# The tile's own layer norm taken in columns through a DRAM round trip, g's parts in one instruction, and a written-out order for the last tile

## The chip, the cores and the metric

One core of one Trainium2 chip runs the whole program. The metric is the device time of one execution in microseconds (us), as the median of several; a profiled execution of the same kernel has a time of its own and a span, from its first to its last instruction.

## The reference

There are 10,000 rows `x` of width 128 and a 10,000 x 10,000 matrix `adj`. Cut to what matters:

```python
h = item_feat @ W_item.T + b_item
x = x + relu(adj @ h + layernorm(x) @ W_user.T + b_user)     # x1
xn = layernorm(x)                                            # the tile's own normalisation
probs = softmax(xn @ gate_w + gate_b); cw = top-2 of probs, 0 elsewhere
x = x + sum_e cw[:, e] * (gelu(xn @ W1[e] + b1[e]) @ W2[e] + b2[e])     # 8 experts, hidden 256
```

The layer norm takes mean and variance over the 128 features of a row and has an eps of 1e-5.

## The kernel before

Everything is held transposed: features lie in the 128 partitions and rows of `x` in columns. The 10,000 rows are cut into 20 tiles of T = 500 columns. One pass of the program multiplies one tile by all of `adj`'s columns, in NPOS = 40 positions. A position 0 to 38 has two blocks of 128 rows of `adj` and three matmuls for each block (high x high, high x low, low x high, since values are split in two fp32r parts), six in all; position 39 has one. ScalarE makes the high part `a_hi` of what the DMA put into `raw` (line 456), VectorE the low part `a_lo` (line 599), TensorE uses both (lines 819 to 821). `raw` and `a_lo` have 8 buffers, `a_hi` has 4, so ScalarE can be at most three positions ahead of TensorE, and SyncE issues the load of a position when TensorE has finished the position eight before it.

The rest of the work, the tail of a tile, is woven into the positions of the next pass, by tables: `tail(i, p)` and `experts(i, p)` on each engine do a step when `p` has the position named at the top of the file (`T_`, `STARTS`, `DOWNS` for TensorE; `A_` for ScalarE; `V_`, `SCALES`, `ADDS` for VectorE; `S_` for SyncE). Positions of 40 and more of a table belong to the following pass. Each engine runs its instructions in the order in which its positions come, and waits at each for semaphores. At one position the order is: the part of `adj`, the tail of this tile, the experts left over from the tile before, the experts of this tile, and the steps of the next tile's `user` normalisation.

The tail of a tile before the change:

- ScalarE takes relu of `acc` into `r_sb` (481), VectorE adds `x_sb` into `x1_sb` (652), TensorE turns `x1_sb` into rows in `ps_v` with four transposes (854, `T_TURN`).
- VectorE takes mean and variance of the rows (612 to 621), GpSimd the power -0.5 (418), VectorE normalises the rows into `xt_sb` with four instructions (625), and TensorE turns them back into columns in `ps_x` with four transposes (827, `T_BACK`).
- ScalarE copies `ps_x` into `xn_hi` (485), VectorE makes `xn_lo` (661), ScalarE copies `ps_x` into `xn_sb` (488), TensorE multiplies that with the gate's weights (863), and the softmax and the ranking of the top two run on VectorE and ScalarE (668 to 710, 491). The weights go to DRAM (495) and come back, spread over all partitions, as `spread_sb` (374).
- For each expert TensorE makes `ps_z` (878 to 880, three matmuls for each of two halves; called up below), ScalarE gelu in `g_sb` (505) and its high part `g_hi` (511), VectorE the low part `g_lo` (718), TensorE the product into `ps_y` (844 to 846, six matmuls; called down below), and VectorE the scaled `t_sb` (727) and the sum `o_sb` (741). `g_sb` has two buffers of two halves.

The `user` normalisation of the next tile's `x` already goes the other way: its means and roots are turned by one small VectorE transpose, stored in DRAM (`u_moments_rows`, 474) and read back spread over all partitions (353, 354), and the columns are normalised in place by a subtraction and a product (642, 644).

After the twentieth pass there is no further pass to weave into: all engines go through the same tables with no `adj` work between.

## Time and profile before

| | |
|---|---|
| time, median of 3 runs | 1610.36 us (1608.63 to 1611.47) |
| profiled execution: its time | 1609.19 us |
| its span | 1607.3 us |
| TensorE matmul busy (PE) | 1585.5 us, 99% |
| TensorE weight loads busy (PEld) | 1310.9 us, 82% |
| VectorE busy (DVE) | 1497.5 us, 93% |
| ScalarE busy (ACT) | 1247.6 us, 78% |
| mean granted TensorE clock | 0.998 |

In a profile the engines are PE and PEld (TensorE's matmuls and weight loads), DVE (VectorE), ACT (ScalarE), POOL (GpSimd) and SP (SyncE); a name with q is an engine's queue, at which it issues DMAs. A busy time counts a stretch in which two matmuls overlap once, and one matmul of 500 columns lasts longer than the distance to the next; so what an instruction costs the engine is read from the starts of its neighbours in the timeline.

### The profile page before, as it was taken

To read this page: it belongs to the slowest core of one execution; us is meant where nothing else is said; L and a number is where in the kernel's file an instruction comes from. 1 tells how busy PE (TensorE), PEld (TensorE's weight loads), DVE (VectorE), ACT (ScalarE), POOL (GpSimd) and SP (SyncE) were. 2 spreads that over 40 slices of the span, in tenths; PEclk is the share of its full clock that TensorE was granted. 3 is DMA by queue.
4 is the path that set the end of the run, shared out by engine and by line. 5 is a ranking of instruction groups with operands and counts; after the bars stand their busy time and mean duration, and the time that the engine had idled before them with its cause. 6 is when DMAs were issued, how large, how long until landed. Compare 5 with 4: busy or idle time off the path is not lost.

```text
span 1607.3 us, 26715 instructions
## 1 busy us (share of the span) xinstructions
PE 1585.5 (99%) x7165; PEld 1310.9 (82%) x7165; DVE 1497.5 (93%) x2328; ACT 1247.6 (78%) x1597; POOL 86.0 (5%) x63
## 2 busy tenths in 40 slices
PE   8999999999999999999999999999999999999996
PEld 7878888888888888888888888888888888888875
DVE  6989999999999999999999999999999999999987
ACT  5777877787878787878787777878787878787765
POOL 2000000000000000000000000000000000000000
PEclk9999999999999999999999999999999999999999
DMA  9999898989898989898989889898989898989851
GB/s 375 359 335 324 271 333 283 318 287 319 285 318 286 316 280 320 289 318 291 314 298 305 301 301 304 297 317 288 315 278 338 265 333 269 332 278 324 281 176 65
DMA packets 159974, 477.75 MB, mean 297 GB/s; under 512 B 22817, under 2 KB 55458, under 8 KB 159954
## 3 DMA queue, kind: packets, MB, share of 16 engines
q1 hardware_dynamic: 150816, 469.37, 86.0%
q10 hardware_dynamic: 8306, 5.84, 1.1%
q0 software_dynamic: 832, 2.30, 0.4%
q8 instruction: 10, 0.16, 0.0%
q14 instruction: 10, 0.08, 0.0%
HBM read 471.66 MB, written 5.78 MB: 297 GB/s over the span
## 4 chain that ended last, share of the span: by engine, by line
issue 92%; PE 4%; POOL 2%; DVE 1%; ACT 1%; DMA 0%; POOLq 0%; ACTq 0%; DVEq 0%
POOL moments_sb L418 2%; PE acc L819 1%; PE acc L821 1%; PE acc L820 1%; ACT g_sb L505 0%; DVE g_lo L718 0%; DMA w_item_sb<-in_w_itemT 0%; PE ps_v L790 0%; DVE o_sb L741 0%; PE ps_y L790 0%; PE ps_g L790 0%; ACT a_hi L456 0%; PE ps_z L790 0%; PE ps_y L844 0%; DVE a_lo L599 0%
## 5 line engine op out<-in xcount | busy, mean ns | idle before, releaser
L456 ACT ACTIVATE a_hi<-raw 128x1000 fp32r<-128x1000 f32 (+1 forms) x800 | 811.8, 1027 | 257.1 <-PE acc L821 202.3
L599 DVE TENSOR_TENSOR a_lo<-raw,a_hi 128x1000 fp32r<-128x1000 f32 x780 | 916.2, 1193 | 57.8 <-ACT a_hi L456 56.3
L819 PE MATMUL acc<-a_hi,h_hi 128*128 128x500 f32 x1560 | 610.4, 391 | 2.3 <-DVE a_lo L599 1.5
L821 PE MATMUL acc<-a_hi,h_lo 128*128 128x500 f32 x1560 | 608.1, 390 | 0.0
L820 PE MATMUL acc<-a_lo,h_hi 128*128 128x500 f32 x1560 | 605.6, 388 | 0.0
L819 PEld LDWEIGHTS acc<-a_hi,h_hi 128*128 128x128 f32 x1560 | 293.5, 188 | 62.8 <-issue 3.5
L820 PEld LDWEIGHTS acc<-a_lo,h_hi 128*128 128x128 f32 x1560 | 294.1, 189 | 59.3
L821 PEld LDWEIGHTS acc<-a_hi,h_lo 128*128 128x128 f32 x1560 | 293.3, 188 | 59.8
L505 ACT ACTIVATE g_sb<-ps_z,b_sb 128x500 f32<-128x500 f32 x320 | 197.9, 670 | 38.9 <-PE ps_y L846 30.3
L718 DVE TENSOR_TENSOR g_lo<-g_sb,g_hi 128x500 fp32r<-128x500 f32 x320 | 201.8, 672 | 7.2 <-ACT g_hi L511 7.2
L511 ACT ACTIVATE g_hi<-g_sb 128x500 fp32r<-128x500 f32 x320 | 179.3, 611 | 0.0
L878 PE MATMUL ps_z<-xn_hi,w_hi 128*128 128x500 f32 x320 | 126.8, 396 | 1.6 <-ACT g_sb L505 1.6
L844 PE MATMUL ps_y<-g_hi,w_hi 128*128 128x500 f32 x312 | 122.2, 392 | 5.0 <-DVE g_lo L718 5.0
L880 PE MATMUL ps_z<-xn_hi,w_lo 128*128 128x500 f32 x320 | 125.0, 391 | 0.0
L879 PE MATMUL ps_z<-xn_lo,w_hi 128*128 128x500 f32 x320 | 124.7, 390 | 0.0
L845 PE MATMUL ps_y<-g_lo,w_hi 128*128 128x500 f32 x312 | 122.0, 391 | 0.0
L846 PE MATMUL ps_y<-g_hi,w_lo 128*128 128x500 f32 x312 | 121.7, 390 | 0.0
L727 DVE SCALAR_TENSOR_TENSOR t_sb<-ps_y,b_sb,spread_sb 128x500 f32<-128x500 f32 x156 | 114.1, 732 | 0.0
L418 POOL TENSOR_TENSOR moments_sb<-var_sb,power_sb 128x4 f32<-128x4 f32 x20 | 37.8, 1888 | 1234.4 <-DVE var_sb L621 1234.4
L741 DVE TENSOR_TENSOR o_sb<-o_sb,t_sb 128x500 f32<-128x500 f32 x140 | 94.2, 673 | 1.0
L844 PEld LDWEIGHTS ps_y<-g_hi,w_hi 128*128 128x128 f32 x312 | 59.2, 190 | 19.4 <-issue 7.4
L878 PEld LDWEIGHTS ps_z<-xn_hi,w_hi 128*128 128x128 f32 x320 | 60.3, 188 | 17.2 <-issue 4.4
(126 smaller groups left out, 878.0 us busy)
## 6 DMA issues: line engine op xcount, KB each, us to landing
raw<-in_adj_main SPq DMA_DIRECT2D x780, 500.0 KB, 5.3
spread_sb<-scales SPq DMA_DIRECT2D x160, 250.0 KB, 6.1
xr_sb<-in_xR SPq DMA_DIRECT2D x20, 256.0 KB, 5.4
x_sb<-in_xT SPq DMA_DIRECT2D x20, 250.0 KB, 5.0
xr_sb<-u_moments_rows SPq DMA_DIRECT2D x20, 250.0 KB, 5.4
r_sb<-u_moments_rows SPq DMA_DIRECT2D x20, 250.0 KB, 6.7
out<-o_sb ACTq DMA_DIRECT2D x20, 250.0 KB, 5.9
items<-in_itemT SPq DMA_DIRECT2D x13, 384.0 KB, 8.2
```

The source lines that it names most:

```text
L456: nc.scalar.activation(a_hi[q][0:rows, 0:cols], raw[s][0:rows, 0:cols], ACT.Copy).then_inc(hi_ready, 1)
L505: nc.scalar.activation(g_sb[e % 2][j][:, :], ps_z[j][:, 0:T], ACT.Gelu, bias=b1_sb[:, e * HH + j:e * HH + j + 1]).then_inc(gelu_ready, 1)
L511: nc.scalar.activation(g_hi[e % 2][j][:, :], g_sb[e % 2][j][:, :], ACT.Copy).then_inc(g_hi_ready, 1)
L599: nc.vector.tensor_tensor(low, whole, val(high), ALU.subtract).then_inc(lo_ready, 1)
L718: nc.vector.tensor_tensor(g_lo[e % 2][j][:, :], g_sb[e % 2][j][:, :], val(g_hi[e % 2][j][:, :]), ALU.subtract).then_inc(g_lo_ready, 1)
L819: nc.tensor.matmul(acc[:, 0:T], w_hi, m_hi, start=(k == 0), stop=False)
L820: nc.tensor.matmul(acc[:, 0:T], w_hi, m_lo, start=False, stop=False)
L821: last = nc.tensor.matmul(acc[:, 0:T], w_lo, m_hi, start=False, stop=False)
L844: nc.tensor.matmul(y, w2_hi[:, cols], hi, start=(j == 0), stop=False)
L878: nc.tensor.matmul(ps_z[j][:, 0:T], w1_hi[:, at:at + P], xn_hi[:, :], start=True, stop=False)
L879: nc.tensor.matmul(ps_z[j][:, 0:T], w1_hi[:, at:at + P], xn_lo[:, :], start=False, stop=False)
L880: nc.tensor.matmul(ps_z[j][:, 0:T], w1_lo[:, at:at + P], xn_hi[:, :], start=False, stop=True).then_inc(z_done, 1)
```

## The change

The tile's own normalisation goes the way of the `user` one. VectorE transposes the 32 columns of means and roots (`turned_sb[1]`), ScalarE stores them in a new DRAM tensor `t_moments_rows` (`A_MOMENTS`), SyncE reads the means into `xt_sb` and the roots into `r_sb`, spread over all partitions (`S_TAIL`), and VectorE makes `xn_sb` from `x1_sb` in two instructions (`V_XN`). The four row instructions, TensorE's four transposes back and ScalarE's copy into `xn_sb` are gone; `xn_hi` and `xn_lo` are made from `xn_sb`. The two halves of `g_sb`, `g_hi` and `g_lo` become one tile each, and high and low part take one instruction of 1000 columns in place of two of 500. The tables have new positions. The first two DMAs on ScalarE's queue change places. For the last tile `g` gets four buffers, in `raw`, `a_lo` and `a_hi`, and each engine's order after the last pass is written out.

```diff
-T_TURN, T_BACK, T_GATE = 1, 9, 13
-U_DENSE = 38
-STARTS = (15, 21, 24, 30, 37, 39, 43, 49)
-DOWNS = (21, 28, 35, 38, 43, 45, 51, 55)
-SCALES = (34, 37, 40, 42, 48, 51, 55, 61)
-ADDS = (36, 40, 41, 42, 51, 54, 58, 62)
+T_TURN, T_GATE = 0, 15
+U_DENSE = 37
+STARTS = (13, 20, 23, 28, 34, 39, 42, 48)
+DOWNS = (20, 24, 35, 40, 42, 45, 51, 58)
+SCALES = (35, 36, 38, 42, 48, 52, 59, 60)
+ADDS = (36, 37, 41, 46, 50, 56, 60, 61)
-S_SPREAD = (34, 34, 34, 35, 42, 45, 49, 54)
+S_SPREAD = (36, 36, 36, 36, 43, 44, 46, 50)
-A_RELU, A_NORM, A_XN, A_EXP, A_SEND, A_STORE, A_USER, A_FFN, A_SCALED = 2, 13, 15, 17, 28, 30, 17, 4, 6
-V_X1, V_STATS, V_NORM, V_LO, V_USTATS, V_UTURN, V_UNORM, V_SCALED = 2, 4, 6, 12, 10, 14, 33, 6
-S_USER = 26
-V_LOGITS, V_PROB, V_COMPARE, V_RANK, V_WEIGHT = 15, 18, 20, 22, 24
+A_RELU, A_MOMENTS, A_NORM, A_EXP, A_SEND, A_STORE, A_USER, A_FFN, A_SCALED = 1, 5, 13, 22, 28, 30, 17, 4, 5
+V_X1, V_STATS, V_NORM, V_XN, V_LO, V_USTATS, V_UTURN, V_UNORM, V_SCALED = 1, 2, 3, 11, 13, 8, 11, 31, 5
+S_TAIL, S_USER = 13, 25
+V_LOGITS, V_PROB, V_COMPARE, V_RANK, V_WEIGHT = 20, 22, 23, 24, 25
...
+            def spread_tail(i, p):
+                if p == S_TAIL:
+                    sp.wait_ge(t_stored, i * 16)
+                    sp.dma_start(xt_sb[:, 0:T], columns(t_moments_rows, 0)).then_inc(t_spread, 16)
+                    sp.dma_start(r_sb[:, :], columns(t_moments_rows, 2)).then_inc(t_spread, 16)
...
+            act.dma_start(w_item_sb[:, :], w_itemT).then_inc(w_item_landed, 16)
             act.dma_start(b_item_raw[0:1, 0:D], b_item).then_inc(b_item_landed, 16)
-            act.dma_start(w_item_sb[:, :], w_itemT).then_inc(w_item_landed, 16)
...
                 if p == V_NORM:
                     dve.wait_ge(t_rstd, i)
-                    normalise(1, xt_sb[0:TQ, :], ps_v[0:TQ, :], t_normed)
+                    since(dve, t_stored, i * 16 - 16)
+                    nc.vector.transpose(turned_sb[1][:, :], moments_sb[1][:, :]).then_inc(t_squared, 1)
+                if p == V_XN:
+                    dve.wait_ge(t_spread, i * 32)
+                    dve.wait_ge(relu_ready, i)
+                    nc.vector.tensor_tensor(xn_sb[:, 0:T], x1_sb[:, 0:T], xt_sb[:, 0:T], ALU.subtract).then_inc(t_less, 1)
+                    dve.wait_ge(t_less, i)
+                    nc.vector.tensor_tensor(xn_sb[:, 0:T], xn_sb[:, 0:T], r_sb[:, :], ALU.mult).then_inc(xn_ready, 1)
...
+            def low(i, e):
+                g, hi, lo = g_places(i)
+                dve.wait_ge(g_hi_ready, expert(i, e) + 1)
+                nc.vector.tensor_tensor(lo[e % len(g)][:, :], g[e % len(g)][:, :], val(hi[e % len(g)][:, :]),
+                                        ALU.subtract).then_inc(g_lo_ready, 1)
```

The written-out end, TensorE's part of it (`rest` is tile 19's leftover, NB tile 20):

```diff
+            tail(NB, T_TURN)
+            down(rest, 3)
+            down(rest, 4)
+            up(rest, 6)
+            down(rest, 5)
+            up(rest, 7)
+            down(rest, 6)
+            tail(NB, T_GATE)
+            up(NB, 0)
+            down(rest, 7)
+            up(NB, 1)
+            up(NB, 2)
+            down(NB, 0)
...
+            down(NB, 5)
+            down(NB, 6)
+            down(NB, 7)
```

VectorE's order there begins with the sum of `rest`'s expert 2, then `x1`, the statistics, the scaling of 3, the small transpose, the scaling of 4; after `V_XN` come the scaling of 5, the logits, the sum of 5 and `xn_lo`. It ends with the scaling and sum of 6 and the scaling and sum of 7. ScalarE's has relu, gelu and high part of 5, the store of the moments, and alternates gelu and high part for the rest.

## Rows read from the trace of the kernel before

**Rows 1.** Waits of the steady passes: engine, line, releaser; us, times, longest.
```profile
PEld acc L819 <- DVE a_lo L599: 1.0, 4, 0.4
```
**Rows 2.** Timeline of TensorE at two pass ends: start us, duration, instruction.
```profile
777.14 1.00 PE L834 MATMUL acc<-xn_sb,w_user_sb 128*128 128x500 f32 x2
...
854.89 1.00 PE L834 MATMUL acc<-xn_sb,w_user_sb 128*128 128x500 f32 x2
```
**Rows 3.** Timeline of TensorE around the four transposes back.
```profile
797.46 0.39 PE L821 MATMUL acc<-a_hi,h_lo 128*128 128x500 f32 x1
797.69 0.60 PE L827 MATMUL ps_x<-ident_sb,xt_sb 128*128 128x128 f32 x4
798.04 0.47 PE L878 MATMUL ps_z<-xn_hi,w_hi 128*128 128x500 f32 x1
798.36 0.39 PE L879 MATMUL ps_z<-xn_lo,w_hi 128*128 128x500 f32 x1
```
**Rows 4.** Timeline of VectorE in the same pass.
```profile
782.38 1.26 DVE L718 TENSOR_TENSOR g_lo<-g_sb,g_hi 128x500 fp32r<-128x500 f32 x2
...
789.52 1.36 DVE L625 TENSOR_SCALAR xt_sb<-ps_v,moments_sb 128x128 f32<-128x128 f32 x4
...
839.57 0.68 DVE L642 TENSOR_TENSOR xn_sb<-x_sb,xr_sb 128x500 f32<-128x500 f32 x1
```
**Rows 5.** Costliest groups of the page: busy, mean ns of one, idle before.
```profile
L456 ACT ACTIVATE a_hi<-raw 128x1000 fp32r<-128x1000 f32 (+1 forms) x800 | 811.8, 1027 | 257.1 <-PE acc L821 202.3
L599 DVE TENSOR_TENSOR a_lo<-raw,a_hi 128x1000 fp32r<-128x1000 f32 x780 | 916.2, 1193 | 57.8 <-ACT a_hi L456 56.3
...
L505 ACT ACTIVATE g_sb<-ps_z,b_sb 128x500 f32<-128x500 f32 x320 | 197.9, 670 | 38.9 <-PE ps_y L846 30.3
...
L727 DVE SCALAR_TENSOR_TENSOR t_sb<-ps_y,b_sb,spread_sb 128x500 f32<-128x500 f32 x156 | 114.1, 732 | 0.0
```
**Rows 6.** Waits of SyncE's queue, whole span: us, times, longest.
```profile
SPq L105 <- DMA scales<-cwT_sb: 14.1, 17, 1.6
```
**Rows 7.** Timeline: the weights' store and the first reads of it.
```profile
827.87 0.53 ACTq L495 DMA_DIRECT2D scales<-cwT_sb  x1
...
833.12 1.39 SPq L374 DMA_DIRECT2D spread_sb<-scales  x3
```
**Rows 8.** DMA issue of the page: KB each, median us to landing.
```profile
r_sb<-u_moments_rows SPq DMA_DIRECT2D x20, 250.0 KB, 6.7
```
**Rows 9.** Windows, after the last pass: length, busy (count), then clock, DMA.
```profile
1555.80:1573.70 17.90, 13.82 (x59) 10.15 (x58) 15.16 (x40) 11.03 (x19) 1.37 (x1) 0.91 0.04 15
```
**Rows 10.** Timeline after the last pass.
```profile
1557.82 0.47 PE L878 MATMUL ps_z<-xn_hi,w_hi 128*128 128x500 f32 x1
...
1568.61 1.06 PE L863 MATMUL ps_g<-gate_w_sb,xn_sb 128*128 128x8 f32 x8 [0.99 <-ACT xn_sb L488]
...
1573.71 0.51 PE L878 MATMUL ps_z<-xn_hi,w_hi 128*128 128x500 f32 x1
...
1581.36 0.54 ACTq L495 DMA_DIRECT2D scales<-cwT_sb  x1
...
1583.32 0.80 SPq L374 DMA_DIRECT2D spread_sb<-scales  x2
...
1601.94 0.39 PE L846 MATMUL ps_x<-g_hi,w_lo 128*128 128x500 f32 x1
...
1604.68 0.35 ACTq L516 DMA_DIRECT2D out<-o_sb  x1
```
**Rows 11.** DMA issues in the stretch after the last pass.
```profile
spread_sb<-scales SPq DMA_DIRECT2D x9, 250.0 KB, 3.3
```
**Rows 12.** Timeline of the start.
```profile
0.75 0.55 ACTq L434 DMA_DIRECT2D xn_sb<-in_b_item  x1
...
1.33 0.37 ACTq L435 DMA_DIRECT2D w_item_sb<-in_w_itemT  x1
...
5.56 1.65 PE L790 MATMUL ps_v<-w_item_sb,items 128*128 128x128 f32 x6 [5.56 <-DMA w_item_sb<-in_w_itemT]
```

More of the change, by code:

```diff
@@ L184, in build @@
         with ExitStack() as whole:
-            g_sb = [[whole.enter_context(nc.sbuf_tensor(f"g_sb{s}_{j}", [P, T], fp32)) for j in range(HH)] for s in range(2)]
-        g_lo = [[sb(f"g_lo{s}_{j}", [P, T], fp32r) for j in range(HH)] for s in range(2)]
+            g_sb = [whole.enter_context(nc.sbuf_tensor(f"g_sb{s}", [P, HH * T], fp32)) for s in range(2)]
+        g_lo = [sb(f"g_lo{s}", [P, HH * T], fp32r) for s in range(2)]
         with ExitStack() as first_pass:
@@ L288, in build @@
         b_item_raw = xn_sb
-        landing = [g_sb[0][0], g_sb[0][1], t_sb[1], x1_sb, o_sb]
+        landing = [g_sb[0][:, 0:T], g_sb[0][:, T:2 * T], t_sb[1], x1_sb, o_sb]
         def columns(rows, n):
@@ L540, in _ @@
                 one_pass(i, True, True)
-            for p in range(NPOS):
-                tail(NB, p)
-                experts(NB - 1, p + NPOS)
-                if p == A_STORE:
-                    finish(NB)
-                experts(NB, p)
-            for p in range(NPOS, 2 * NPOS):
-                experts(NB, p)
+            rest = NB - 1
+            tail(NB, A_RELU)
+            gelu(rest, 5)
+            high(rest, 5)
+            tail(NB, A_MOMENTS)
+            gelu(rest, 6)
+            high(rest, 6)
+            gelu(rest, 7)
+            tail(NB, A_NORM)
+            high(rest, 7)
+            tail(NB, A_EXP)
+            gelu(NB, 0)
+            high(NB, 0)
+            gelu(NB, 1)
+            tail(NB, A_SEND)
+            high(NB, 1)
+            gelu(NB, 2)
+            finish(NB)
+            high(NB, 2)
+            gelu(NB, 3)
+            high(NB, 3)
+            gelu(NB, 4)
+            high(NB, 4)
+            gelu(NB, 5)
+            high(NB, 5)
+            gelu(NB, 6)
+            high(NB, 6)
+            gelu(NB, 7)
+            high(NB, 7)
             finish(NB + 1)
@@ L731, in add @@
[L731 to L742 removed]
+                    low(i, STARTS.index(p - V_SCALED))
@@ L744, in one_pass @@
+                if p in SCALES:
+                    scale(i, SCALES.index(p))
+                if p in ADDS:
+                    add(i, ADDS.index(p))
             def one_pass(i, with_tail, with_finish):
@@ L764, in _ @@
                 one_pass(i, True, True)
-            for p in range(NPOS):
-                tail(NB, p)
-                experts(NB - 1, p + NPOS)
-                add(NB - 1, p + NPOS)
-                experts(NB, p)
-                add(NB, p)
-            for p in range(NPOS, 2 * NPOS):
-                experts(NB, p)
-                add(NB, p)
+            rest = NB - 1
+            add(rest, 2)
+            tail(NB, V_X1)
+            tail(NB, V_STATS)
+            scale(rest, 3)
+            tail(NB, V_NORM)
+            scale(rest, 4)
+            add(rest, 3)
+            low(rest, 5)
+            low(rest, 6)
+            add(rest, 4)
+            tail(NB, V_XN)
+            scale(rest, 5)
+            tail(NB, V_LOGITS)
+            add(rest, 5)
+            tail(NB, V_LO)
+            low(rest, 7)
+            scale(rest, 6)
+            tail(NB, V_PROB)
+            add(rest, 6)
+            tail(NB, V_COMPARE)
+            tail(NB, V_RANK)
+            tail(NB, V_WEIGHT)
+            low(NB, 0)
+            scale(rest, 7)
+            add(rest, 7)
+            low(NB, 1)
+            low(NB, 2)
+            scale(NB, 0)
+            scale(NB, 1)
+            add(NB, 0)
+            low(NB, 3)
+            scale(NB, 2)
+            add(NB, 1)
+            low(NB, 4)
+            add(NB, 2)
+            scale(NB, 3)
+            low(NB, 5)
+            add(NB, 3)
+            scale(NB, 4)
+            add(NB, 4)
+            low(NB, 6)
+            scale(NB, 5)
+            add(NB, 5)
+            low(NB, 7)
+            scale(NB, 6)
+            add(NB, 6)
+            scale(NB, 7)
+            add(NB, 7)
         @block.tensor
@@ L822, in adj_step @@
                 last.then_inc(adj_used, 1)
-            def back(rows, done):
-                for q in range(Q):
-                    last = nc.tensor.transpose(ps_x[:, q * TQ:(q + 1) * TQ], rows[0:TQ, q * D:(q + 1) * D],
-                                               ident_sb[0:TQ, 0:TQ])
-                last.then_inc(done, 1)
             def user(i, p):
```

160 lines of the change are left out of this document (77 added, 83 removed).

## The prediction

> **What bounds the kernel now.** I read first the busy shares of the page: TensorE 99%, VectorE 93%. A busy share alone doesn't name the bound, so the waits of the steady passes come next. Between the first and the last pass end TensorE's weight loads lose 1.0 us in all to a missing low part [rows 1]; VectorE's lateness costs nothing. So a steady pass is as long as TensorE's queue. Its length is the distance of the `user` matmuls at two pass ends, 854.89 - 777.14 = 77.75 us [rows 2]. One matmul of 500 columns costs 0.227 us from start to start (797.46 to 797.69 is 0.23), though it is shown 0.39 long [rows 3]; six of them, a position or an up or a down, cost 1.36. What TensorE no longer has to do shortens each pass; what the other engines save shortens nothing there. After the last pass it is different: in the first 17.9 us TensorE is busy 13.82, and the clock granted is 0.91 of full speed on the mean [rows 9]. There chains of waits decide. That end lasts from 1555.8 to the span's end at 1607.3, 51.5 us.
>
> **The steady passes: what goes.** The four transposes back start at 797.69, the next two matmuls at 798.04 and 798.36 [rows 3]. From 797.46 to 798.36 are 0.90 us, in which two matmuls alone would take 0.454. So the transposes cost 0.446 us a pass. They go in 19 passes outside the end: 19 x 0.446 = 8.5 us. The gate's, the turn's and the experts' matmuls stay, only at other positions. Here a rule of the Trainium skill can be weighed: the page "TensorE: Matmul & The Clock Gate" (section "Back-to-back issue gap") gives some 81 ns for each weight load and matmul of 128 columns in a stream. By it the estimate would be 4 x 0.081 x 19 = 6.2 us; no row here shows the 81 ns, and the row's 0.446 for four stands.
>
> VectorE, per pass: the four row instructions go (1.36 us [rows 4]); a subtraction and a product come, like the pair of `user`, 2 x 0.68 us [rows 4], and a small transpose (0.1 to 0.2 us); eight pairs of low parts become single instructions, 1.26 against 1.19 us [rows 4, 5], 0.56 saved. The net is -0.4 us (0.1 to 0.2 of the 1.36 is overlap with neighbours), about what TensorE's pass loses, so VectorE is as loaded as before. ScalarE loses a copy and gains a DMA issue of 0.53 us (as in [rows 7]); it is at 78% and its total is free.
>
> **The new waits in a pass.** I walk the new tables with position 0 of TensorE at time 0, a position, an up and a down at 1.36 us each. The chain is: relu, `x1`, turn at 1.4 to 1.8; statistics to 3.6; power on GpSimd; the small transpose at 5.7; ScalarE reaches position 5 at 6.5 (at position 3 it waits until 3.4 for `down` of expert 3, since `g_sb` has two buffers) and issues the store at about 7.5. What the store takes under load is the unknown. [Rows 7] bound it from above: 833.12 - 827.87 = 5.25 us for the like store of the weights, and SyncE was held by that one in 17 cases by 0.8 us on the mean [rows 6], so it is not much less. From below the quiet end gives 1583.32 - 1581.36 = 1.96 us [rows 10]. I take 5.25, as it is under the same traffic: 12.75. SyncE comes to position 13 when TensorE has ended position 5, at 12.9, so its wait costs it next to nothing, and the loads of `raw` queued behind are not late. It issues the two reads at 13.3 and 13.65; the root's takes 6.7 us in the median [rows 8]: 20.35. VectorE, loaded as it is, ends `a_lo` of position 11 at about 20.8. So the wait of `V_XN` just fits. Queued behind it is everything of VectorE, first `a_lo` 12, which by the walk is ready 1.1 to 1.5 us before TensorE wants it. The cover of the round trip is thus 0.45 + about 1.1 = 1.5 us.
>
> The second tight place is `DOWNS[1]` = 24, while the low part it needs stands at VectorE's position 25, behind `a_lo` 25 and `V_WEIGHT`. TensorE would start that down at 50.3. VectorE's queue from position 18 on, where it waits for ScalarE until 32.1, holds 8 `a_lo` at 1.11 us from start to start (1.19 long [rows 5] with the overlap of 0.08), three more pieces of `low`, scale and sum, and the gate's five steps (an estimate of 3.5 us together, from the starts of their neighbours in the same pass): it ends at 49.8. There are 0.5 us left. At the other places I find a microsecond or more: `up` 6 at 5.9 has its gelu at 4.6, `up` 5 at 75.9 its at 72.2. So I cost the new order at nothing in the likeliest case, with 0 to +0.5 us a pass as the range; a gain is excluded, since TensorE already waits for nothing.
>
> SyncE's two more reads are 0.5 MB on top of some 23 MB a pass, 2%; the DMA engines are busy 0.90 of the time there, and `raw` has its eight buffers in front. I cost it at nothing, and the landing of the reads above already stands in the traffic.
>
> **The start.** `w_item` moves from the second to the first place of ScalarE's queue, 1.33 to 0.75 us [rows 12]. TensorE's first matmul waits for it until 5.56; from there it is in a chain with TensorE busy nearly all of the first pass. Up to 0.58 us gained, nothing if another load is last; I take 0.5.
>
> **The end.** Before, the first `up` of tile 20 starts at 1573.71 and the last matmul at 1601.94 [rows 10]. New (in the times of the old run): the turn is over when TensorE's next matmul starts, 1557.8 [rows 10], the statistics come next in VectorE's written order, 1.5 us from 1558.15, and GpSimd's power takes 1.4 (its whole busy time in [rows 9]): 1561.1. But ScalarE is free for the store only after gelu and high part of expert 5. Gelu waits for `down` 3, which takes the matmul's place of 1557.8 and ends 1.6 later with its latency, 1559.45. Two halves of gelu at 0.62 from start to start (0.67 long) and a high part of 1.03 [rows 5] make 1561.75. The store takes 1.96 [rows 10]: 1563.7. The second read is issued at 1564.0 and lands 3.3 later [rows 11]: 1567.3. Subtraction and product to 1568.8, gate to 1569.9 (1.06 [rows 10]), logits 0.6, the sum of 5 0.6, `xn_lo` 0.6: 1571.9. So `up` 0 comes 1.8 us earlier although the round trip is long, since the old chain stood behind other work. From there TensorE has 17 pieces of 1.36 us (8 up, 9 down), 23.1 us; before it had 16, 21.8 us, and took 1602.3 - 1573.7 = 28.6. In the new order ScalarE needs per expert 2 x 0.62 + 1.03 = 2.3 us and VectorE 1.19 + 0.73 + 0.6 = 2.5, both under TensorE's 2.72, and four buffers keep them apart. What is left is the first gelu (table load and gelu to 1575.5, high and low part to 1577.6) against which `down` 7, `up` 1 and `up` 2 are set, and some small waits; by the walk the last down starts at 1596.35 and ends at 1597.8. After it come one scaling and one sum in place of a scaling and two sums: 1.6 us to 1599.4, and from the issue of the output 2.65 us as before (1607.3 - 1604.68 [rows 10]): 1602.05. That is 5.25 us less. TensorE still waits for the gate and for `xn_lo`, some 3 us with the gate's small matmuls between, as in the stretch whose mean clock was 0.91 [rows 9]. I expect the lower level of the two (1.2 GHz) again in `up` 0, which puts the first gelu 0.7 us later. So 4.6 us are left.
>
> **The sum.** 8.5 + 0.5 + 4.6 = 13.6 us. The profiled execution took 1609.2 us (span 1607.3, 1.9 around it), so the one after would take 1595.6, its span 1593.7. The median stands 1.2 above the profiled one: 1596.8. I say 1596.5.
>
> **The rivals.**
> - *The round trip is longer than its cover (slower side).* Place: `V_XN` at position 11, VectorE's whole queue behind it, TensorE's `a_lo` next. It decides from 1.5 us more than worked out above (a root landing after 21.9); each us beyond costs 19 us in all. To lose against before it needs 13.6 / 19 = 0.7 us more, 2.2 in all. With 3 us more: 1.5 x 19 = 28 lost, 1611. For it: the reads land between 6 and 8 us under load, and terms are in series. Against: 5.25 is an upper bound. 9%.
> - *The low part of expert 1 is late.* Place: TensorE's `down` 1. VectorE 0.9 us later than my walk costs 0.4 x 18 = 7 us: 1604. For it: VectorE is 93% busy and the margin is the thinnest. 14%.
> - *The end gives nothing:* a read that lands 2 us later, and half clock for longer, eat 4.6 us: 1601. 10%.
> - *The transposes cost their whole duration.* Were the 0.60 us shown for the group [rows 3] all TensorE's time, 19 x 0.60 = 11.4 would go in place of 8.5: 1593.9. Against it speaks the start of the next matmul 0.35 us after theirs. The page "TensorE: Matmul & The Clock Gate" of the Trainium skill (section "Part 4: PE-mode transpose") has "~275 ns" for one in a kernel; four in series, an estimate by it, would be 1.1 us a pass and 21 us in all. 3%.
> - *The change doesn't do what it says:* TensorE's time is freed and VectorE becomes the bound, 1605 to 1609, as VectorE's total shrinks no faster than the pass. Against: at 93% it has some 5 us of a pass idle. 3%.
>
> The forecast itself, 1592 to 1600, has 61%.
>
> **How the numbers follow.** The range leaves out most of the first rival, the upper end of the last and what the end may bring beyond the forecast: 1591.5 to 1606.5. Faster by over 0.2% (3.2 us, about what a measurement tells from no change) is all below 1607.1: forecast, third, fourth, most of the second and part of the last, 0.86. Same: 0.06. Slower, above 1613.6 or nearly: 0.08.
>
> **What would show it.** The distance between `user` matmuls should be 77.3 us; TensorE's waits in the passes still near nothing. Were the first rival true, VectorE's `xn_sb` from `x1_sb` would show a wait for the read of `t_moments_rows` in most passes and TensorE one for `a_lo`. The second shows as TensorE at `ps_y` waiting for `g_lo` once a pass. In the end, `up` 0 should start some 14 us after the first matmul behind the turn (1571.9 - 1557.8), and the last matmul some 26.5 us after `up` 0; a later `up` 0 makes the third rival. If VectorE's idle time falls to nothing while TensorE's waits grow, the last is true.

## The result and the profile after

The changed kernel takes 1598.41 us in the median of 6 runs (1597.69 to 1600.52), the old one 1609.62 (1608.63 to 1611.47, 6 runs). The ratio is 0.9933 with a 95% interval of 0.9923 to 0.9944: 11.2 us faster. The profiled execution of the changed kernel took 1598.9 us, its span is 1596.9 where the old span was 1607.3, so the two traces differ by 10.4 us. The forecast was 13.6 us between profiled executions and 1596.5 as the time.

The page of the changed kernel, busy time and share by engine:

```profile
PE 1575.2 (99%) x7085; PEld 1304.3 (82%) x7085; DVE 1491.0 (93%) x2148; ACT 1225.2 (77%) x1419; POOL 68.5 (4%) x63
```

TensorE has 80 matmuls fewer and VectorE 180 instructions fewer, yet the shares are what they were. So the shares don't say where the 10.4 us come from; marks on TensorE's queue do. As the mark of a pass I take the start of the pass's last `adj` matmul, L810 before and L892 after. Timeline of TensorE before, at the ends of passes 0, 1 and 19 (start us, duration, instruction):

```profile
85.96 0.78 PE L810 MATMUL acc<-a_hi,h_hi 128*128 128x500 f32 x1
...
155.51 0.79 PE L810 MATMUL acc<-a_hi,h_hi 128*128 128x500 f32 x1
...
1555.14 0.79 PE L810 MATMUL acc<-a_hi,h_hi 128*128 128x500 f32 x1
```

The same after, with the `user` pair (L909) of two passes:

```profile
87.09 0.38 PE L892 MATMUL acc<-a_hi,h_hi 128*128 128x500 f32 x1
...
158.09 0.39 PE L892 MATMUL acc<-a_hi,h_hi 128*128 128x500 f32 x1
...
773.59 1.00 PE L909 MATMUL acc<-xn_sb,w_user_sb 128*128 128x500 f32 x2
...
850.80 1.00 PE L909 MATMUL acc<-xn_sb,w_user_sb 128*128 128x500 f32 x2
...
1547.92 0.39 PE L892 MATMUL acc<-a_hi,h_hi 128*128 128x500 f32 x1
```

One thing has to be set right first. The matmul that follows the `user` pair takes 0.62 us to the next start, not 0.23 (774.04 to 774.66 after, 777.59 to 778.21 before). Before, the mark itself is that matmul; after, the pair stands a position earlier and the slow step lies ahead of the mark. So 0.39 us moves from behind the mark to ahead of it, in pass 0 as a loss that is none, in the end as a gain that is none. With that:

| stretch | before | after | difference | forecast |
|---|---|---|---|---|
| pass 0, to its mark | 85.96 | 87.09 | +1.13, less 0.39: +0.74 | -0.5 |
| pass 1 | 69.55 | 71.00 | +1.45 | -0.45 |
| passes 2 to 19 | 1399.63 | 1389.83 | -9.80 | -8.0 |
| mark to the span's end | 52.16 | 48.98 | -3.18, plus 0.39: -2.79 | -4.6 |
| sum | | | -10.4 | -13.6 |

The steady pass is 850.80 - 773.59 = 77.21 us, where it was 77.75 [rows 2]. The window of the steady passes after (length; busy time and count of PE, PEld, DVE, ACT and POOL; clock, DMA share, GB/s), and behind it the waits there (engine, line, releaser: us, times, longest), to set beside [rows 1]:

```profile
160.00:1547.00 1387.00, 1387.00 (x6199) 1148.86 (x6198) 1318.62 (x1888) 1081.17 (x1239) 52.58 (x36) 1.00 0.91 310
```
```profile
PEld acc L901 <- DVE a_hi L640: 0.2, 1, 0.2
```

TensorE has no gap in 1387 us. [Rows 1] shows one of two such lines of the old kernel; the other is

```profile
PEld acc L810 <- DVE a_lo L599: 1.6, 7, 0.2
```

The two cost nearly nothing: 16 of the old kernel's 18 passes from mark 1 to mark 19 are 77.75 us apart and two are 77.84 and 77.85, so the old pass too was as long as TensorE's queue.

The new round trip (store, two reads, `V_XN`) and the thin margin of `down` 1 in one steady pass, whose mark is at 775.79:

```profile
783.16 0.54 ACTq L502 DMA_DIRECT2D t_moments_rows<-turned_sb  x1
...
790.83 0.35 SPq L356 DMA_DIRECT2D xt_sb<-t_moments_rows  x1
791.24 0.42 SPq L357 DMA_DIRECT2D r_sb<-t_moments_rows  x1
...
797.94 0.67 DVE L697 TENSOR_TENSOR xn_sb<-x_sb,xt_sb 128x500 f32<-128x500 f32 x1
...
815.65 0.74 DVE L764 SCALAR_TENSOR_TENSOR t_sb<-ps_y,b_sb,spread_sb 128x500 f32<-128x500 f32 x1 [0.89 <-PE ps_y L922]
...
825.86 1.16 DVE L756 TENSOR_TENSOR g_lo<-g_sb,g_hi 128x1000 fp32r<-128x1000 f32 x1
...
827.68 0.39 PE L920 MATMUL ps_y<-g_hi,w_hi 128*128 128x500 f32 x1
```

With position 0 at 777.37, the reads leave at 13.5 and 13.9 (walked: 13.3 and 13.65) and `V_XN` starts at 20.6 (walked: 20.8). The store goes out at 5.8, not 7.5. The page gives 5.6 us from issue to landing of the root's read, not 6.7:

```profile
r_sb<-t_moments_rows SPq DMA_DIRECT2D x20, 250.0 KB, 5.6
```

With this median as an estimate the root is there at 796.84, 1.1 us ahead of `V_XN`, which waits for nothing. SyncE never waits for the store in these passes; it does so twice in the whole span, 0.3 us in pass 1 and 2.6 us in the end:

```profile
SPq L356 <- DMA t_moments_rows<-turned_sb: 2.9, 2, 2.6
```

The low part of expert 1 ends at 827.02, 0.66 us ahead of its down product (walked: 0.5).

Pass 1 is another matter. SyncE, VectorE and TensorE there, after:

```profile
95.28 0.49 PE L901 MATMUL acc<-a_hi,h_hi 128*128 128x500 f32 x1 [0.61 <-DVE a_lo L640]
...
98.94 0.33 SPq L356 DMA_DIRECT2D xt_sb<-t_moments_rows  x1
99.69 0.33 SPq L357 DMA_DIRECT2D r_sb<-t_moments_rows  x1
...
106.00 0.68 DVE L697 TENSOR_TENSOR xn_sb<-x_sb,xt_sb 128x500 f32<-128x500 f32 x1 [1.61 <-DMA r_sb<-t_moments_rows]
...
108.65 0.49 PE L901 MATMUL acc<-a_hi,h_hi 128*128 128x500 f32 x1 [2.08 <-DVE a_lo L640]
```

In a steady pass TensorE has ups and downs of the previous tile between its `adj` products (at positions 0 to 18), and VectorE gets ahead meanwhile. Pass 1 has no previous tile. From 100 to 125 us TensorE is idle 2.08 us, all in this last wait; before, it was idle 0.00 there.

The end after, in order of time:

```profile
1559.43 0.68 DVE L697 TENSOR_TENSOR xn_sb<-x_sb,xt_sb 128x500 f32<-128x500 f32 x1 [1.25 <-DMA r_sb<-t_moments_rows]
...
1560.88 1.06 PE L936 MATMUL ps_g<-gate_w_sb,xn_sb 128*128 128x8 f32 x8 [0.79 <-DVE xn_sb L699]
...
1563.89 0.76 PE L948 MATMUL ps_z<-xn_hi,w_hi 128*128 128x500 f32 x1 [1.95 <-issue]
...
1577.57 0.74 DVE L764 SCALAR_TENSOR_TENSOR t_sb<-ps_y,b_sb,spread_sb 128x500 f32<-128x500 f32 x1 [1.37 <-DMA spread_sb<-scales]
...
1588.55 0.47 PE L920 MATMUL acc<-a_hi,w_hi 128*128 128x500 f32 x1 [0.70 <-DVE a_lo L756]
...
1591.02 0.47 PE L920 MATMUL ps_x<-a_hi,w_hi 128*128 128x500 f32 x1 [0.86 <-DVE a_lo L756]
...
1592.22 0.38 PE L922 MATMUL ps_x<-a_hi,w_lo 128*128 128x500 f32 x1
...
1594.13 0.35 ACTq L535 DMA_DIRECT2D out<-o_sb  x1
```

`up` 0 follows the first matmul behind the turn (1550.20) by 13.7 us; 14 was forecast. From `up` 0 it is 28.3 us to the start of the last matmul and 28.7 to its end; some 26.5 was forecast. That is where the end fell short.

### The profile page after: what moved, and what is told of

Its sections match the earlier page's. It is cut to its first block, busy times and chain, and to the rows that moved or that the text cites. A ratio compares the mean times of both kernels' runs of the same rounds, so it can differ in the third digit from the quotient of the medians.

```text
span 1596.9 us, 26046 instructions
## 1 busy us (share of the span) xinstructions
PE 1575.2 (99%) x7085; PEld 1304.3 (82%) x7085; DVE 1491.0 (93%) x2148; ACT 1225.2 (77%) x1419; POOL 68.5 (4%) x63
## 4 chain that ended last, share of the span: by engine, by line
issue 93%; PE 2%; DMA 2%; POOL 1%; DVE 1%; ACT 0%; SPq 0%; POOLq 0%; DVEq 0%; ACTq 0%
POOL moments_sb L431 1%; DMA raw<-in_adj_main 1%; PE acc L901 0%; PE acc L903 0%; PE acc L902 0%; DMA spread_sb<-scales 0%; DVE t_sb L764 0%; DMA r_sb<-t_moments_rows 0%; DVE o_sb L775 0%; ACT a_hi L469 0%; DVE a_lo L640 0%; DVE a_lo L756 0%; DMA t_moments_rows<-turned_sb 0%; SPq L334 0%; PE ps_y L872 0%
## 5 line engine op out<-in xcount | busy, mean ns | idle before, releaser
L901 PE MATMUL acc<-a_hi,h_hi 128*128 128x500 f32 x1560 | 617.7, 396 | 6.3 <-DVE a_lo L640 5.5
L517 ACT ACTIVATE g_sb<-ps_z,b_sb 128x500 f32<-128x500 f32 x304 | 188.0, 669 | 61.9 <-PE ps_y L922 59.7
L756 DVE TENSOR_TENSOR g_lo<-g_sb,g_hi 128x1000 fp32r<-128x1000 f32 x152 | 181.0, 1191 | 5.2 <-ACT g_hi L523 5.1
L523 ACT ACTIVATE g_hi<-g_sb 128x1000 fp32r<-128x1000 f32 x152 | 156.3, 1028 | 0.1
L922 PE MATMUL ps_y<-g_hi,w_lo 128*128 128x500 f32 x304 | 118.2, 389 | 0.0
L431 POOL TENSOR_TENSOR moments_sb<-var_sb,power_sb 128x4 f32<-128x4 f32 x20 | 21.0, 1052 | 1211.7 <-DVE var_sb L662 1211.7
L949 PEld LDWEIGHTS ps_z<-xn_lo,w_hi 128*128 128x128 f32 x320 | 60.6, 189 | 12.2
```

Of the source, the lines that this page charges most:

```text
L517: nc.scalar.activation(g[e % len(g)][:, j * T:(j + 1) * T], ps_z[j][:, 0:T], ACT.Gelu, bias=b1_sb[:, e * HH + j:e * HH + j + 1]).then_inc( ...
L523: nc.scalar.activation(hi[e % len(g)][:, :], g[e % len(g)][:, :], ACT.Copy).then_inc(g_hi_ready, 1)
L756: nc.vector.tensor_tensor(lo[e % len(g)][:, :], g[e % len(g)][:, :], val(hi[e % len(g)][:, :]), ALU.subtract).then_inc(g_lo_ready, 1)
L901: nc.tensor.matmul(acc[:, 0:T], w_hi, m_hi, start=(k == 0), stop=False)
L949: nc.tensor.matmul(ps_z[j][:, 0:T], w1_hi[:, at:at + P], xn_lo[:, :], start=False, stop=False)
```

## The experiments

All but one start from the changed kernel. The steady pass is taken from the marks of passes 1 to 19 in one execution, where it nearly always repeats to 0.01 us as long as nothing waits. All times but the last kernel's are of single runs, the profiled ones, and are compared with the profiled execution of the changed kernel, 1598.9 us. Its parts outside the steady passes vary from one execution to the next, as shown below. The old kernel ran beside them in 1609.3 to 1610.0 us.

### The transposes back again

```diff
+                if p == 9 and not is_last(i):
+                    for q in range(Q):
+                        nc.tensor.transpose(ps_x[0:TQ, q * D:(q + 1) * D], x1_sb[:, q * TQ:(q + 1) * TQ], ident_sb[:, :])
```

> The changed kernel with four 128x128 transposes of x1 into the bank of the z product put back on TensorE at position 9 of passes 1 to 19, where the old kernel turned the normalised tile back; nobody reads or waits for them, so they cost TensorE's time alone. My account (TensorE's own work sets the steady pass, and the removed transposes were worth 0.446 us): the steady pass goes from 77.21 to 77.66 us, and the run by about 8.5 us, from 1598.4 to 1607. Rival (each transpose costs its whole 0.15 us duration, 0.60 for four): 77.81 us, and 1610. Rival (the gain came from a wait in the old path around the transposes, not from their own time): below 77.4 us, under 4 us in all.

1606.33 us, 7.4 more. Two marks in a row:

```profile
779.72 0.39 PE L892 MATMUL acc<-a_hi,h_hi 128*128 128x500 f32 x1
...
857.36 0.39 PE L892 MATMUL acc<-a_hi,h_hi 128*128 128x500 f32 x1
```

77.64 us, 0.43 more than without them. My account stands: the transposes cost TensorE what the starts around them show, 0.353 for the four and 0.085 more for the matmul behind them. 0.353 / 4 is 0.088 us each. The page "TensorE: Matmul & The Clock Gate" of the Trainium skill (section "Back-to-back issue gap") says some 81 ns, which comes near that but leaves out the slower matmul behind. The "~275 ns" of the same page of the Trainium skill (section "Part 4: PE-mode transpose") is three times what the rows show. But the old pass is 77.75: 0.11 us a pass, 2.0 us in 18, came from something else.

### A wait that is met, and g in two parts

The first puts eight waits a pass back on TensorE, the second also the 16 instructions that the merging took away.

```diff
                 for j in range(HH):
+                    if j:
+                        pe.wait_ge(g_lo_ready, expert(i, e) + 1)
```

> The changed kernel with one more semaphore wait on TensorE ahead of the second half of each expert's down product, for a count that has always been reached: eight more waits a pass, as many as the old kernel had. The steady pass got 0.535 us shorter where the transposes explain 0.446. Theory A (each wait costs TensorE about 11 ns even when its count is reached): the steady pass goes from 77.21 to 77.30 us, the run by 1.6 us. Theory B (a wait that is met costs nothing, and the 0.09 came from elsewhere): 77.21 us, no change.

```diff
...
+                for j in range(HH):
+                    part = slice(j * T, (j + 1) * T)
+                    dve.wait_ge(g_hi_ready, i * (E * HH) + (HH * (e - E) + j + 1))
+                    nc.vector.tensor_tensor(lo[e % len(g)][:, part], g[e % len(g)][:, part], ...
...
```

> The changed kernel with the high and the low part of g made in two instructions of 500 columns each again, each with a wait and a signal of its own, and TensorE waiting for each low part, as in the old kernel; all else as changed. It puts 8 instructions a pass on ScalarE and 8 on VectorE back, and TensorE's 8 waits. Theory A (the merged instructions give TensorE the 0.09 us a pass by its waits): steady pass 77.30 us, VectorE's busy share up by about 1 us a pass with no new wait. Theory B (it comes from elsewhere): 77.21 us. Rival: VectorE gets so late that down 1, with its margin of 0.66 us, waits in each pass: over 77.5 us, with a wait of ps_y for g_lo in the rows.

1599.78 and 1599.12 us; the marks are 77.21 us apart in both (854.23 - 777.02, and within a hundredth 852.95 - 775.73). Theory B holds twice: a wait whose count is reached costs TensorE nothing that can be seen, and the merging of g's parts brings no time in the steady pass, though VectorE's busy time is 1502.1 us with two parts and 1491.0 with one. The 0.11 us stay open as to their cause. The starts show where they sit: over six passes the ordinary step of TensorE is 0.2270 us on the mean in the old kernel and 0.2267 in the changed one, which over 327 steps a pass makes 0.10 us. Most of it comes from eleven places of the old pass, ten with a step of 0.234 or 0.235 us and one of 0.254; five of them lie in an `up`. The changed kernel has three places of 0.234 or 0.235. Why these steps are longer no run tells; the new positions of the work in a pass were not put back one by one.

### The first load

The old kernel, with only the item weight's transfer ahead of the item bias's.

```diff
+            act.dma_start(w_item_sb[:, :], w_itemT).then_inc(w_item_landed, 16)
             act.dma_start(b_item_raw[0:1, 0:D], b_item).then_inc(b_item_landed, 16)
-            act.dma_start(w_item_sb[:, :], w_itemT).then_inc(w_item_landed, 16)
```

> The old kernel with nothing changed but the order of the two transfers that ScalarE's queue issues first (the item weight before the item bias). My account gave 0.5 us for it in the whole run: first matmul at 5.0 instead of 5.56 us and the end of pass 0 at 85.5 instead of 85.96 us. Rival, from the trace after (first matmul earlier by 0.53, end of pass 0 later by 1.13 us): the first pass is set by the landings of the raw item tiles, so the end of pass 0 does not come earlier, 85.9 us or later, and the run is the same within 0.5 us.

1609.39 us, the mark of pass 0 at 86.11. TensorE starts 0.77 us earlier than before and waits twice more, for low parts that are late because ScalarE waits for raw tiles to land:

```profile
4.79 1.65 PE L790 MATMUL ps_v<-w_item_sb,items 128*128 128x128 f32 x6 [4.79 <-DMA w_item_sb<-in_w_itemT]
...
15.73 0.46 PE L819 MATMUL acc<-a_hi,h_hi 128*128 128x500 f32 x1 [0.64 <-DVE a_lo L599]
...
19.28 0.47 PE L819 MATMUL acc<-a_hi,h_hi 128*128 128x500 f32 x1 [1.10 <-DVE a_lo L599]
```

0.64 + 1.10 is more than twice what was won. The rival stands: the first 20 us go by the landings of the raw tiles (the fourth is converted at 16.71 before and 16.86 here), and an earlier first matmul only waits for them.

### How much cover has the round trip?

Reads at SyncE's position 14, then 16, for 13.

```diff
-    S_TAIL, S_USER = 13, 25
+    S_TAIL, S_USER = 14, 25
```

> The changed kernel with the two reads of the tile's moments one position later on SyncE's queue (14 for 13), so 1.36 us later; all else the same. The question is how much of the round trip's time is covered in the steady pass. In the changed kernel the spread rows are there about 1.1 us before V_XN's turn on VectorE, and the low parts of adj run 1.36 us ahead of TensorE, 2.5 us of cover in all. Theory (cover 2.5 us): V_XN waits up to 0.3 us a pass, the steady pass stays at 77.21 us; only pass 1, where the cover is gone, gets up to 1.4 us longer. Rival (the cover is the 1.5 us that the forecast worked out, or less): the steady pass is 77.3 to 78 us and the run 2 to 14 us longer, with waits of acc for a_lo in each pass.

1614.96 us, 16 more, 3.1 of it in pass 1; the steady pass is 78.04 on the mean of passes 3 to 19, between 77.3 and 78.7. My theory of 2.5 us of cover falls. One read issue and `V_XN` of a pass whose mark is at 783.85, and behind them the waits over passes 3 to 19:

```profile
801.63 0.36 SPq L356 DMA_DIRECT2D xt_sb<-t_moments_rows  x1
...
807.24 0.68 DVE L697 TENSOR_TENSOR xn_sb<-x_sb,xt_sb 128x500 f32<-128x500 f32 x1 [1.15 <-DMA r_sb<-t_moments_rows]
```
```profile
DVE xn_sb L697 <- DMA r_sb<-t_moments_rows: 32.1, 17, 2.5
...
PEld acc L901 <- DVE a_lo L640: 21.8, 47, 1.1
```

The reads leave 17.78 us behind the mark, where they left 15.04 (790.83 - 775.79): one position on SyncE is 2.74 us later here, since a `down` of the previous tile (798.12 to 799.48 in this trace) lies between the two `adj` positions whose ends free the two slots. `V_XN` then waits 32.1 / 17 = 1.89 us, so its slack had been 0.85; the pass loses 0.83, so the low parts ran 1.06 ahead. The cover is 1.9 us, 0.4 more than the forecast's 1.5 and 0.6 less than I had then read off one pass.

> The changed kernel with the two reads of the tile's moments at position 16 for 13, about 5 us later in SyncE's order (behind the raw transfers of three more positions); all else the same. Theory (cover 2.5 us in the steady pass): V_XN waits about 4 us a pass, TensorE about 2.5 of it for a_lo, steady pass 79.7 us, the run 45 us longer, about 1643. By the forecast's cover of 1.5 us: 3.5 us a pass, 63 us, 1661. Rival (the round trip was never near the path, everything queued behind V_XN has slack too): within 5 us of the changed kernel.

1687.01 us, the steady pass 81.9. Waits, and the window of the steady passes:

```profile
DVE xn_sb L697 <- DMA r_sb<-t_moments_rows: 75.6, 16, 5.6
...
PEld acc L901 <- DVE a_lo L640: 56.7, 24, 4.2
```
```profile
238.00:1486.00 1248.00, 1203.61 (x5259) 988.89 (x5258) 1119.36 (x1604) 919.57 (x1054) 44.81 (x31) 0.98 0.87 294
```

`V_XN` waits 4.7 us a pass and TensorE is idle 44.4 us of 1248, 2.9 in a pass of 81.9; but the pass is 4.7 us longer. Most of the rest is the clock: 0.98 of full speed on the mean, where the changed kernel has 1.00. The idle time is 15 waits of 2.3 to 3.8 us, and behind each of them five to nine steps take some 0.42 us in place of 0.227, 18.7 us in all or 1.2 in a pass. The last 0.6 us a pass is not assigned. All three expectations were too low; I had left the clock out.

### The thin margin of down 1

```diff
-DOWNS = (20, 24, 35, 40, 42, 45, 51, 58)
+DOWNS = (20, 23, 35, 40, 42, 45, 51, 58)
```

> The changed kernel with the down product of expert 1 one position earlier on TensorE (23 for 24). In the changed kernel it starts at 827.68 us and its low part of g ends at 827.02: a margin of 0.66 us. One position earlier it would start at 826.31. Theory (the low part of g keeps its time, TensorE waits the difference): 0.7 us a pass of ps_y for g_lo, steady pass 77.9 us, the run 13 us longer, about 1611. Rival (waiting TensorE shifts the adj products behind it and their low parts come earlier against them, so that the time is won back within the pass): below 77.4 us, less than 3 us longer.

1614.18 us, the steady pass 78.07. The wait is one a pass, in the place named (waits, then one of them in the timeline):

```profile
PEld ps_y L920 <- DVE g_lo L756: 17.5, 17, 1.0
```
```profile
833.91 0.49 PE L920 MATMUL ps_y<-g_hi,w_hi 128*128 128x500 f32 x1 [0.61 <-DVE g_lo L756]
```

The pass is 0.85 us longer, against 0.7 expected; nothing is won back within the pass. One position is all there is between the table in use and 15 us.

### Pass 1

```diff
-                if p == V_XN:
+                if p == V_XN + (1 if isinstance(i, int) and i == 1 else 0):
```

> The changed kernel with V_XN at VectorE's position 12 for 11 in pass 1 alone, so that the low parts of adj of position 12 go ahead of its wait for the round trip in the one pass that has no ups and downs left over to cover it. In the changed kernel pass 1 takes 71.0 us against 69.55 before, though it has 0.45 us less of transposes and 1.36 less of down products (one is done in the next pass instead); TensorE waits 2.08 us for a_lo in one piece behind V_XN. Theory (the round trip's wait in VectorE's queue is what TensorE waits for there): that wait falls to about 1 us and pass 1 to about 70 us, the run is 1 us shorter. Rival (the low parts only come late for another reason, DMA or ScalarE): pass 1 is as long as before this edit, and so is the run.

1597.99 us. The wait in question:

```profile
109.50 0.50 PE L901 MATMUL acc<-a_hi,h_hi 128*128 128x500 f32 x1 [0.34 <-DVE a_lo L640]
```

2.08 us became 0.34, and pass 1 took 69.31 us (88.31 to 157.62), 1.7 less. The run is only 0.9 shorter than the changed kernel's: its end was 0.5 shorter and its pass 0 1.2 us longer, two parts that this edit doesn't touch. That start varies, 86.5 to 88.3 in the traces of the changed kernel and its descendants; pass 1 varies too. Seven traces with `V_XN` at 11 in pass 1 and nothing added there (the changed kernel, the two on g, `down` 1, and the three on the end below) have 70.2 to 73.4 us, 71.7 on the mean, with `V_XN` waiting 0.8 to 2.7 us. The old kernel had 69.55 in both its traces. The 69.31 lies below all seven, and the kernel that carries this edit on (below) has 69.07. So the theory stands.

### The end: the clock, the four places of g, two orders

```diff
             down(rest, 6)
+            fill(4)
             tail(NB, T_GATE)
+            fill(8)
             up(NB, 0)
```

> The changed kernel with 12 matmuls of 500 columns that nobody reads put into TensorE's waits of the end: 4 before the gate and 8 after it, so that TensorE does not idle ahead of up 0. In the changed kernel up 0 and down 7 ran at half the clock there (12 steps of 0.42 us, 5.1 us for what takes 2.7). Theory A (TensorE sets the end, the half clock is paid in full): with a full clock the end is 2.4 us shorter, less up to 0.5 for the fill running over. Theory B (from about 13 us later VectorE's queue sets the end: scale 0 waits 1.37 us for its landing, then VectorE works to the last add with under 1 us of gaps): the clock stays at 2.4 GHz and the end is shorter by 0.5 us at most.

1601.46 us, but its first two passes were slow: its mark of pass 19 is at 1551.34, 3.4 us later than the changed kernel's. From there to the span's end are 48.06 us against 48.98. Window from 1555 to 1575 us, this kernel first, the changed one second:

```profile
1555.00:1575.00 20.00, 17.98 (x79) 13.67 (x79) 16.59 (x36) 13.53 (x18) 1.01 (x1) 1.00 0.14 40
```
```profile
1555.00:1575.00 20.00, 16.30 (x62) 12.97 (x63) 15.13 (x29) 13.80 (x19) 0.00 (x0) 0.83 0.13 45
```

The clock stays at 2.4 GHz, and the end is 0.9 us shorter in this pair of traces: between Theory B's 0.5 and the 1.9 that Theory A leaves after the fill. But the end varies by as much without the fill. The six other traces above that leave it as in the changed kernel (transposes, waits, reads at 14 and at 16, `down` 1, pass 1) have 48.0 to 48.8 us, with 6 to 13 slow steps behind `up` 0, and the 48.98 is the longest of the seven. So TensorE's 2.3 us at 1.2 GHz cost the end between nothing and 0.9 us. What does set it shows in all eleven traces with four places for g, the two below among them: scale 0 starts 28.3 to 31.3 us behind the mark, and the span ends 19.2 to 19.5 us after that start each time. That is Theory B.

```diff
-            return (last_g, last_hi, last_lo) if is_last(i) else (g_sb, g_hi, g_lo)
+            return (g_sb, g_hi, g_lo)
```

> The changed kernel with the last tile's experts in the same two places for g as in all other passes, instead of the four of raw, a_hi and a_lo; orders and all else as changed, so ScalarE may only run two experts ahead of the down products at the end. Theory (the four places are what lets the gelus go ahead, most of the gain of the end): the stretch from the last adj product to the end of the span goes from 48.98 us to 51 or more. Rival (the written orders alone do it): 49 to 49.5 us.

1606.06 us, and 54.2 us from mark to end, 5.2 more than with four places. Waits from 1566 us on:

```profile
PE ps_z L948 <- ACT g_sb L517: 3.8, 5, 0.8
...
PE ps_x L920 <- DVE g_lo L756: 2.1, 1, 2.1
```

With two places each gelu waits for a down product and each `up` for that gelu, 0.77 us five times over, and the last down 2.1. The old end, 51.8 us by the same measure (52.16 - 0.39), was better than this one. So the four places carry the end; these written orders without them lose 2.4 us against the old ones.

```diff
             scale(rest, 5)
+            tail(NB, V_LO)
             tail(NB, V_LOGITS)
             add(rest, 5)
-            tail(NB, V_LO)
...
             high(NB, 0)
+            tail(NB, A_SEND)
             gelu(NB, 1)
-            tail(NB, A_SEND)
```

> The changed kernel with two places exchanged in the written orders of the end. VectorE takes the low part of the normalised tile ahead of the logits, not behind them and an add (it may start at about 1561.5, starts at 1563.12, and up 0 follows at 1563.89); ScalarE issues the store of the expert weights ahead of gelu 1 and not behind it (cwT is ready at 1569.2, the store goes out at 1571.14, the spread rows land for scale 0 at 1577.57, after a wait of 1.37 us). Theory B of the fill run (VectorE's queue from scale 0 on sets the end): scale 0 starts 1.4 to 1.9 us earlier and the span ends 1.3 to 1.9 us earlier. Theory A (TensorE from up 0 on sets it): the same 1.6 us by the earlier up 0, with the waits of down 5 and down 7 as they are. Rival (both only turn waits into others, the table load between exp and gelu 0 holds the chain): under 0.5 us.

1599.25 us, 50.65 us from mark to end: 1.7 worse than the longest of the seven ends above, where all theories had it better or equal. ScalarE and TensorE:

```profile
1569.32 0.53 ACTq L509 DMA_DIRECT2D scales<-cwT_sb  x1
1569.95 1.24 ACT L517 ACTIVATE raw<-ps_z,b_sb 128x500 f32<-128x500 f32 x2 [3.62 <-DVE t_sb L764]
...
1570.68 0.79 PE L948 MATMUL ps_z<-xn_hi,w_hi 128*128 128x500 f32 x1 [4.30 <-ACT raw L517]
```

The store has a second wait that I had overlooked, for the last scaling of the previous tile (`since(act, scaled, ...)` beside `cwT_ready`). That scaling stands behind the low part of expert 0 in VectorE's order and ended at 1569.2, and gelu 1 was queued behind the store. The other half of the edit did what it was for: `up` 0 starts 1.4 us behind the gate's start, 3.0 before. Scale 0 starts 31.3 us behind the mark, and the span ends 19.4 later.

### Both mended

`V_XN` at 12 in pass 1, `V_LO` ahead of the logits, and the store where its waits are met:

```diff
-            low(NB, 0)
             scale(rest, 7)
+            low(NB, 0)
             add(rest, 7)
...
             gelu(NB, 1)
-            tail(NB, A_SEND)
             high(NB, 1)
+            tail(NB, A_SEND)
```

> The changed kernel with what the runs so far point to. In pass 1 alone V_XN stands one position later (12), as in the run that did only that (pass 1 took 69.3 us there, 70.2 to 73.4 in eight kernels that have it at 11). At the end VectorE takes the low part of the normalised tile ahead of the logits (up 0 followed the gate by 1.4 us so, 3.0 without it) and the scale of the previous tile's last expert ahead of the low part of expert 0; ScalarE stores the expert weights behind the high part of expert 1, since that store waits for this very scale, and holding gelu 1 behind it cost 4.3 us of TensorE's time. Theory: pass 1 gains 1.5 to 2.5 us, the end 1 to 1.5 us (47.5 to 48 us from the last adj product to the end of the span): 1594.5 to 1596, a ratio to the old kernel of 0.990 to 0.992. Rival (the end stays bound by VectorE's queue from the landing of the spread rows on, and the gain of pass 1 is the chance of one run): 1597 to 1598.5, no gain over the changed kernel.

1596.06 us in the median of 5 runs (1595.50 to 1597.12), the old kernel beside it 1610.38 (9 runs); ratio 0.9914, 95% interval 0.9900 to 0.9927. The changed kernel had 1597.69 to 1600.52, so the two sets of times don't overlap. The expected 1594.5 to 1596 was missed by 0.06. Pass 1 took 69.07 us, and from 100 us on the trace shows no matmul of `adj` waiting for a low part; the end took 47.85. `up` 0 and scale 0 there:

```profile
1560.62 0.46 PE L948 MATMUL ps_z<-xn_hi,w_hi 128*128 128x500 f32 x1 [0.35 <-issue]
...
1574.59 1.42 DVE L764 SCALAR_TENSOR_TENSOR t_sb<-ps_y,b_sb,spread_sb 128x500 f32<-128x500 f32 x2 [2.46 <-DMA spread_sb<-scales]
```

Scale 0 starts 28.3 us behind the mark at 1546.25, where it started 29.65 behind it in the changed kernel: 1.3 earlier, and the end is 1.1 shorter. That the end follows the landing of the spread rows is what Theory B of the fill run says. Against the seven traces with the changed kernel's end, 48.0 to 49.0, the gain is 0.2 to 1.1. Pass 1 gives 1.9 of the 2.8 us between the two profiled executions.

## Why the prediction was right, and where it was not

The time, 1596.5 with 1591.5 to 1606.5, was 1.9 us too low. The likeliest case is what happened; its terms, one by one:

- *Bound by TensorE's queue, the transposes at 0.446 us.* Right, by the run that puts them back: 0.43. The steady pass gained 0.54, so 18 passes gave 9.8 where their share of the sum was 8.0. The 0.11 a pass beyond the transposes comes neither from the waits nor from the merged parts; 0.10 of it is seen in the steps, and its cause is open.
- *The new waits at nothing in a steady pass.* Right, and for the reason given: walk and trace agree to 0.2 us at the reads and at `V_XN`. The store went earlier and the landing was shorter than taken; neither mattered, because SyncE's slot sets the reads and VectorE's own queue the start of `V_XN`. The cover of 1.5 us is 1.9. The margin of 0.5 at `down` 1 is 0.66, and the edit that uses it up costs 0.85 us a pass for 0.71 us too little, a little more than the second rival has for a late low part. The terms named for VectorE's queue there don't give that margin, though: 32.1 and 8 x 1.11 and 3.5 make 44.5, not 49.8. The trace has a wait in between, 0.89 us for a down product until 815.65, which is 38.3 behind position 0, and the low part ends at 49.65. The end of the walk was right, the sum as written is not. In the first rival, too, 3 us more would make 1596.5 + 28 = 1625, not 1611; nothing else hangs on it.
- *19 passes alike.* Wrong, and the mis-step with most in it. The walk was made for a pass that carries the previous tile's ups and downs; pass 1 has none, and I counted it with the others. The first rival, the round trip longer than its cover, came true in this one pass. I also gave the end one down product more (17 pieces for 16) without taking it out of pass 1, which has three now in place of four. Without new waits pass 1 should take 69.55 - 0.45 - 1.36 = 67.7 us. It took 71.0 in the profiled execution: 3.3 us lost, nearly all of it at two waits, 2.08 us behind `V_XN` and 0.61 at 95.28 for a low part that stood behind GpSimd's power. From start to start, with the slower steps right around them, the two come to 3.2.
- *The start, 0.5 us.* Wrong. The bound "nothing if another load is last" was in the text, and the rows of the raw tiles' waits were not read for it. The swap alone brings the first matmul 0.77 us forward and the end of pass 0 not at all. The changed kernel's pass 0 is 0.7 us longer even so: ScalarE converts the fourth raw tile at 17.38, where it did so at 16.71, and TensorE waits 0.46 and 0.91 us for low parts before 20 us. Its traces and those made from it have 86.5 to 88.3 for the mark, which less 0.39 is 86.1 to 87.9, the old 86.0 and 86.1; in the one with 88.3 TensorE waited 1.8 us until 17.4 and then had steps of 0.42. Why it should land later with the same loads is not settled.
- *The end, 4.6 us.* The mechanism was right (`up` 0 when walked, four places keep the engines apart), the size 2.8 in the profiled execution, which has the longest end of the seven traces alike; in the others it is 3.0 to 3.8. From the walk to `up` 0 nothing is missing; from `up` 0 on 2.2 us are. I had 0.7 for the lower clock, and the runs show nothing to 0.9. The rest is a term that the walk did not have: the spread rows of the weights land at 1577.5 and scale 0 waits 1.37 us for them. From then VectorE has 8 scalings, 8 sums and 5 low parts, and ends the last sum at 1594.1, 16.5 us later, with 0.5 us idle in between, so low parts 6 and 7 come late for their downs (0.70 and 0.86; the expectation of the two orders calls the first of them down 5). I walked VectorE's load per expert, not the time at which it may begin.

What the terms make: +1.2 at the start and +1.9 in pass 1 over the forecast, -1.8 in the steady passes, +1.8 in the end; 3.2 us less gain than the 13.6. The errors were of both signs, and part of the nearness of the time is that.

Of the other rivals, the transposes' whole duration and VectorE as the bound are excluded by the run with the transposes and by a TensorE without gaps. That the end gives nothing is excluded by its 2.8 us: the two traces with the old end have 51.8 and 52.1 us by the same measure, the seven with the new one 48.0 to 49.0.

## What to carry to other kernels

A forecast by one steady pass has to be walked again for the first pass that lacks what overlaps it: cover is other work, and the pass without that work pays the wait in full. Before a DMA issue is moved in an engine's order, list every wait that stands ahead of it, since everything queued behind inherits the latest of them. Where TensorE's queue is without gaps, take its time from the starts of its neighbours, and try thin margins by one position; both places tried here were one position from a loss of 15 us.

## What was not expected of the hardware

- A wait whose count is already reached costs TensorE nothing visible: eight more a pass left the pass at 77.21 us.
- The same idle time does not bring the lower clock at the same moment. Ahead of `up` 0 at the end TensorE idled 1.95 to 1.96 us in nine traces. In six of them the steps behind it are slow at once, in the changed kernel twelve of some 0.42 us; in three some four or five faster steps come first, and in the kernel with eight more waits eight slow ones follow these. In pass 1 a wait of 2.0 us went with a granted clock of 0.93 from 100 to 125 us in one trace, and one of 2.08 with 1.00 in another.
- A read of 250 KB issued in the same place of pass 1 kept `V_XN` waiting between 0.8 and 2.7 us over seven traces, while in their steady passes it kept it waiting once, for 0.06 us.
